# Attention pass: runs of equal destinations marked once in the weighted pass, picks in two bf16 parts, summed and marked by matmuls

## The reference, cut to what matters

```
h = (x @ W).reshape(n, H, C)
a_src, a_dst = sum(h * att_src, -1), sum(h * att_dst, -1)
alpha = leaky_relu(a_src[src] + a_dst[dst], 0.2)
amax  = segment_max(alpha, dst)
ex    = exp(alpha - amax[dst])
out   = segment_sum(h[src] * ex / segment_sum(ex, dst)[dst], dst) + bias
```

## Time and profile before

| what | us |
|---|---|
| median of 3 runs | 10127.84 (10118.32 to 10137.22) |
| span of the profiled execution, first to last instruction | 10186.8 |
| weighted pass in it | 5079 to 6036 |
| attention pass in it | 6126 to 7475 |

### The profile page before, as it was taken

One profiled execution on the slowest core, in us unless ns is written; L12 is line 12 of the kernel. 1 busy time (PEld: TensorE's weight loads), 2 busy tenths in 40 slices (PEclk: granted clock), 3 DMA queues, 4 the chain that ended last, 5 costly groups with the idle time before them and its releaser, 6 DMA issues. The chain is left out here.

```text
span 10186.8 us, 130111 instructions
## 1 busy us (share of the span) xinstructions
PE 5972.5 (59%) x26625; PEld 4680.2 (46%) x26626; DVE 3975.1 (39%) x9144; ACT 2065.8 (20%) x6047; POOL 4999.3 (49%) x5128
## 2 busy tenths in 40 slices
PE   4667666756675667466744673555554564465455
PEld 3556445644564456355633552334443453343344
DVE  4444434443343434344511244556641231222123
ACT  2222222222222212222222233322320000000000
POOL 4554454445445544554455525434326555555655
PEclk8888778877887778787877886767777787787778
DMA  4332332333233322332222215544322222222222
GB/s 122 97 93 89 103 96 84 96 89 98 85 93 93 97 82 84 104 101 86 88 81 72 70 48 188 175 160 157 135 75 85 79 80 84 79 82 76 84 82 77
DMA packets 427779, 980.02 MB, mean 96 GB/s; under 512 B 125761, under 2 KB 205121, under 8 KB 411201
## 3 DMA queue, kind: packets, MB, share of 16 engines
q0 software_dynamic: 245760, 673.51, 22.9%
q1 hardware_dynamic: 124528, 190.17, 5.8%
q10 hardware_dynamic: 57296, 114.45, 3.4%
HBM read 842.61 MB, written 135.14 MB: 96 GB/s over the span
## 5 line engine op out<-in xcount | busy, mean ns | idle before, releaser
L322 POOL DMA_INDIRECT ring<-node_table,idx x4608 | 4474.4, 971 | 4298.1 <-issue 1779.2
L685 PE MATMUL psAT<-ring,S 128*128 128x256 f32 x7600 | 2078.3, 435 | 974.8 <-DVE AGG L847 752.6
L261 DVE SCALAR_TENSOR_TENSOR S<-iota,block_start,dst_f 128x512 f32<-128x512 f32 x1710 | 1280.2, 749 | 2951.4 <-remote 1509.2
L685 PEld LDWEIGHTS psAT<-ring,S 128*128 128x128 f32 x7600 | 1635.6, 221 | 1359.6 <-DVE S L261 717.6
L1026 PE MATMUL psAT<-ring,S 128*128 128x256 f32 x4560 | 1272.9, 440 | 1010.6 <-DVE AGG L1122 679.0
L1026 PEld LDWEIGHTS psAT<-ring,S 128*128 128x128 f32 x4560 | 994.1, 224 | 1293.6 <-issue 983.7
L909 DVE TENSOR_TENSOR ring<-ring,psE 128x256 f32<-128x256 f32 x2560 | 903.4, 415 | 772.6 <-remote 416.3
L779 ACT ACTIVATE ring<-ring 128x256 f32<-128x256 f32 x2560 | 846.3, 408 | 1143.5 <-DVE ring L909 637.5
L1282 POOL DMA_INDIRECT ring<-att_table,idx x512 | 524.0, 1023 | 814.1 <-ACT idx L1480 535.2
L611 PE MATMUL psE<-we_stk,stk 128*128 128x256 bf16 x2560 | 426.8, 302 | 450.8 <-DVE ring L909 217.3
L392 PE MATMUL psAT<-ring,S 128*128 128x256 f32 x1520 | 404.6, 426 | 276.2 <-DVE AGG L474 162.7
(11 more groups left out here) (326 smaller groups left out, 5279.6 us busy)
## 6 DMA issues: line engine op xcount, KB each, us to landing
ring<-node_table,idx POOLq DMA_INDIRECT x4608
rows_table<-ring SPq DMA_DIRECT2D x64, 1072.0 KB
ring<-rows_table ACTq DMA_DIRECT2D x64, 1072.0 KB
stk<-stack_table SPq DMA_DIRECT2D x256, 256.0 KB
node_table<-tab ACTq DMA_DIRECT2D x237, 128.0 KB, 1.9
stack_table<-stk SPq DMA_DIRECT2D x64, 256.0 KB
ring<-att_table,idx POOLq DMA_INDIRECT x512
tT<-in_edge_attr SPq DMA_DIRECT2D x68, 64.0 KB
```

The lines of the kernel that those rows point to most:

```text
L261: nc.vector.scalar_tensor_tensor(S[:, 4 * g:4 * g + 4, :], iota[:, :].unsqueeze(1).to_broadcast([P, 4, P]), block_start[:, bass.ds(blk, 1) ...
L322: nc.gpsimd.indirect_dma_start(ring[:, q, 0:gw], None, table, bass.IndirectOffsetOnAxis(ap=idx[:, q:q + 1], axis=0)).then_inc(gathered[q], 16)
L685: ins = nc.tensor.matmul(psA[:, 0:D], S[:, u, :], ring[:, U * ob + u, 0:D], start=(u == 0), stop=(u == U - 1))
```

## The change

- The marks of the runs are found once, for all 65536 edges, in the weighted pass, and kept in two tables in DRAM. `ends_table` has the destination of every edge that is the last of its run in its tile, and -1 for the others. `run_table` has, for every tile and head, what the scan adds: -1e38 where a run begins, else 0 (8 equal rows for the 8 heads, so 2 MB, written by 8 DMAs). Both are read into `Y` at the start of the attention pass.
- `scan` in the sorted case is the scan alone, from `Y` and from PSUM. The copies, comparisons, the product with `last` and `number` are gone, and PE's two transpositions of `dT` and `lastT` with them.
- The one-hot tiles of `hots` and `further` are made from `run_ends`, so only the last edge of a run is marked in them.
- The picks are two bf16 parts instead of three. A unit of `pick` is 25 matmuls with 8 columns (one that writes the huge negative number everywhere, and per tile one that adds the positive one where a destination is, and one for each part, all into the same 64 columns) instead of 8 with 25.
- `take` is one maximum straight from PSUM and the maximum with `a_max`: 2 instructions instead of 4.
- ACT makes the second `hots` ahead of `exp`.

```diff
@@ attention_pass, sync
+                    sp.dma_start(run_ends, ends_table).then_inc(ends_in, 16)
+                    run_rows = run_table.rearrange("(n q) e -> q n e", q=P)
+                    for n0, n1 in ((0, FIRST), (FIRST, 2 * NG)):
+                        sp.dma_start(edge_runs.rearrange("p (n e) -> p n e", e=P)[:, n0:n1, :],
+                                     run_rows[:, n0:n1, :]).then_inc(runs_in, 16)
                     with sp.Fori(0, NG) as i:
@@ tensor: turn_scores, turn_runs, pick
-                        pe.wait_ge(d16_ready, n + 1)
-                        nc.tensor.transpose(sT, gs[:, P * g:P * g + P], ident[:, :])
-                        nc.tensor.transpose(dT, d16[:, :], ident[:, :]).then_inc(scoresT, 1)
+                        nc.tensor.transpose(sT, gs[:, P * g:P * g + P], ident[:, :]).then_inc(scoresT, 1)
...
-                        nc.tensor.transpose(runT, run[:, :], ident[:, :])
-                        nc.tensor.transpose(lastT, last[:, :], ident[:, :]).then_inc(runsT, 1)
+                        nc.tensor.transpose(runT, run[:, :], ident[:, :]).then_inc(runsT, 1)
...
                             pe.wait_ge(picks_read, c + 1)
+                            nc.tensor.matmul(psV[:, 0:U * PW], ones_b[0:1, :], absent, start=True, stop=False)
                             for u in range(U):
...
-                                ins = nc.tensor.matmul(psV[:, PW * u:PW * u + PW],
-                                                       hot_sets[half if first else 2][:, u, :],
-                                                       picks_b[:, U * half + u, :], start=True, stop=True)
+                                high_low = [picks_b[:, U * half + u, PW * part:PW * part + PW] for part in range(2)]
+                                for part, rhs in enumerate((present, *high_low)):
+                                    ins = nc.tensor.matmul(psV[:, PW * u:PW * u + PW],
+                                                           hot_sets[half if first else 2][:, u, :], rhs,
+                                                           start=False, stop=(u == U - 1 and part == 2))
@@ scalar
                         if picking:
                             hots(2 * n, 0)
+                            hots(2 * n + 1, 1)
                         ahead(i, ob, 1, exp)
-                        if picking:
-                            hots(2 * n + 1, 1)
@@ vector: scan (sorted case), split_picks, take
-                            nc.vector.tensor_tensor(pen[:, :], DT, DTp[:, P - 1:2 * P - 1], ALU.not_equal)
-                            nc.vector.tensor_tensor(last[:, :], DT, DTp[:, P + 1:2 * P + 1], ALU.not_equal)
-                            dve.drain()
-                            nc.vector.tensor_scalar(pen[:, :], pen[:, :], -BIG, None, ALU.mult)
-                            dve.drain()
-                            nc.vector.tensor_tensor_scan(run[:, :], pen[:, :], GT, -BIG, ALU.add, ALU.max)
-                            dve.drain()
-                        nc.vector.tensor_tensor(run[:, :], run[:, :], last[:, :], ALU.mult).then_inc(runs_ready, 1)
-                        number(n + 1)
+                            dve.wait_ge(scoresT, n + 3)
+                            nc.vector.tensor_tensor_scan(run[:, :], own_runs, sT, -BIG, ALU.add, ALU.max
+                                                         ).then_inc(runs_ready, 1)
...
                         nc.vector.tensor_copy(part[0], runs)
-                        nc.vector.tensor_scalar(picks_b[:, :, PW - 1:PW],
-                                                lastT.rearrange("p (t h) -> p t h", h=HEADS)[:, :, 0:1],
-                                                FLAG, None, ALU.mult)
                         dve.drain()
-                        nc.vector.tensor_tensor(rest_f, runs, part[0], ALU.subtract)
-                        dve.drain()
-                        nc.vector.tensor_copy(part[1], rest_f)
-                        dve.drain()
-                        nc.vector.tensor_tensor(part[2], rest_f, part[1], ALU.subtract).then_inc(picks_ready, 1)
+                        nc.vector.tensor_tensor(part[1], runs, part[0], ALU.subtract).then_inc(picks_ready, 1)
...
-                            nc.vector.tensor_reduce(cand[:, :, :], pv[:, :, 0:3 * HEADS].rearrange(
-                                "p u (s h) -> p u h s", s=3), AX.X, ALU.add)
-                            dve.drain()
-                            nc.vector.scalar_tensor_tensor(
-                                cand[:, :, :], pv[:, :, PW - 1:PW].to_broadcast([P, U, HEADS]), FLAG,
-                                cand[:, :, :], ALU.subtract, ALU.add).then_inc(picks_read, 1)
-                            dve.drain()
-                            nc.vector.tensor_reduce(cmax[:, :], cand[:, :, :].rearrange("p u h -> p h u"),
-                                                    AX.X, ALU.max)
+                            nc.vector.tensor_reduce(cmax[:, n, :], pv.rearrange("p u h -> p h u"), AX.X, ALU.max
+                                                    ).then_inc(picks_read, 1)
                             dve.drain()
@@ weighted pass, first work: DVE, PE, SP
+        def find_runs(dve):
+            now, own_fence = numbers[:, :, 0:P], fence[:, :, 1:P]
+            uns = dve.value_load(unsorted_i[0:1, 0:1], min_val=0, max_val=1)
+            dve.wait_ge(numbers_turned, 1)
+            nc.vector.memset(numbers[:, :, P:2 * P], -2.0)
+            nc.vector.tensor_copy(now, turned_numbers)
+            dve.drain()
+            nc.vector.tensor_tensor(ended, now, numbers[:, :, 1:P + 1], ALU.not_equal)
+            dve.drain()
+            with dve.If(uns > 0):
...
+            with dve.Else():
+                nc.vector.memset(fence[:, :, 0:1], -BIG)
+                nc.vector.tensor_scalar(own_fence, ended[:, :, 0:P - 1], -BIG, None, ALU.mult)
+            dve.drain()
+            nc.vector.scalar_tensor_tensor(ended, now, 1.0, ended, ALU.add, ALU.mult)
+            dve.drain()
+            nc.vector.tensor_scalar_add(ended, ended, -1.0).then_inc(ends_made, 1)
+            dve.wait_ge(ends_turned, 1)
+            nc.vector.tensor_copy(now, turned_numbers).then_inc(ends_copied, 1)
+        def store_runs(sp):
+            rows_by_head = run_table.rearrange("(c p h) e -> h p c e", p=P, h=HEADS)
+            sp.wait_ge(ends_made, 1)
+            for h in range(HEADS):
+                sp.dma_start(rows_by_head[h], fence).then_inc(runs_out, 16)
+            sp.wait_ge(ends_copied, 1)
+            sp.dma_start(ends_table.rearrange("p (c e) -> p c e", e=P), numbers[:, :, 0:P]).then_inc(ends_out, 16)
...
```

More of the change, by code:

```diff
@@ L134, in build @@
         ST = stk_f[:, U * P:3 * U * P // 2].bitcast(BF16)
-        run, last, pen = (stk_f[:, n * P:n * P + P] for n in (5, 6, 7))
-        picks = share(MT * (HEADS + 1)).rearrange("p (t h) -> p t h", t=MT)
-        al, cand = (share(U * HEADS).rearrange("p (u h) -> p u h", u=U) for n in range(2))
-        cmax = sb("cmax", [P, HEADS])
+        run, pen = (stk_f[:, n * P:n * P + P] for n in (5, 7))
+        al = share(U * HEADS).rearrange("p (u h) -> p u h", u=U)
+        cmax = share(2 * HEADS).rearrange("p (n h) -> p n h", n=2)
         psE = pb("psE", [P, 4 * 512])
@@ L162, in build @@
         weighed = sem("weighed")
-        d16_ready = sem("d16_ready")
+        numbers_turned, ends_made, ends_turned = sem("numbers_turned"), sem("ends_made"), sem("ends_turned")
+        runs_out, ends_out = sem("runs_out"), sem("ends_out")
+        ends_copied, runs_in, ends_in = sem("ends_copied"), sem("runs_in"), sem("ends_in")
         scoresT = sem("scoresT")
@@ L1220, in attention_pass @@
             offsets = [small2[:, U * n:U * n + U] for n in range(3)]
-            picks_b = scale_row[:, 0:MT * PW // 2].bitcast(BF16).rearrange("p (t w) -> p t w", w=PW)
-            rest_f = flat(picks[:, :, :])[:, 0:P].rearrange("p (t h) -> p t h", h=HEADS)
+            picks_b = scale_row[:, 0:MT * PW].bitcast(BF16).rearrange("p (t w) -> p t w", w=2 * PW)
+            edge_runs = Y[:, 0:2 * NG * P]
+            run_ends = Y[:, 2 * NG * P:2 * NG * P + NT]
+            marks, ones_b = (rows[:, 1, P // 2 * n:P // 2 * n + P // 2].bitcast(BF16) for n in range(2))
+            present, absent = marks[:, 0:PW], marks[0:1, PW:PW + U * PW]
+            FIRST = 4
             FLAG = 2.0 ** 126
@@ L1303, in _ @@
                     sp.sem_inc(octet_free, NO)
+                    sp.wait_ge(ends_in, 16)
+                    sp.wait_ge(runs_in, 32)
                     loads(sp)
@@ L1553, in _ @@
                     load(0, 1)
+                    act.wait_ge(ends_in, 16)
                     hots(0, 0)
@@ L1854, in _ @@
                     dve.drain()
-                    number(0)
+                    dve.wait_ge(ends_in, 16)
+                    dve.wait_ge(runs_in, 32)
                     for n in range(2):
@@ L2433, in turned_weight, with turn_numbers @@
```

(39 more changed lines are left out.)

47 lines of the change are left out of this document (21 added, 26 removed).

## The result

The changed kernel takes 10055 us (median of 4 runs) against 10123 for the kernel before, run beside it: ratio 0.9934, 95% interval 0.991 to 0.9957, some 67 us less. 10031 had been predicted. One thing has to be known for all that follows: the chips were of two kinds. On one the kernel before takes 9950 to 10125 us (the first pair and e4 to e7, e10, e11), on the other 7785 (e0 to e3, e8, e9). I call them the slow kind and the quick kind, and compare inside a kind only. Runs that stand on different chips of one kind are compared by their ratios to the kernel before, which ran beside each of them.

A forecast was written before the change was run, and what follows sets the result against it. DVE's program, run nearly serially, was taken to bound the attention pass. Scan and split -57, takes -49, picks +11, second hots -5, weighted pass +3 gave -97 us: 10127.84 - 97 = 10031 us, range 9975 to 10100.

The forecast's parts named there:

- The bound: Attention loop: DVE's program, run nearly serially, sets the pace, its 687 busy us and 244 of waits making 931 of 1175.
- Scan and split, 57 us: DVE in picking steps: shorter scan and split save 2.6 us in first and 1.2 in second steps, over 15 turns.
- freed time turns into waits: Rival, attention loop: PE's sums are late whenever runs are turned, scan and split give nothing; -40 us, 10088; 16%.
- Takes and picks, 49 - 11 + 5 = 43 us: Attention loop: shorter takes on DVE gain 49 us, PE's longer picks lose 11, second hots ahead of exp gain 5.
- the rival of 0.096 us each: PE's picks: weight loads can't overlap, a unit's pick takes 2.4 us instead of 0.36; 10152 us; 9%.
- The third rival: DVE's attention loop, about 100 instructions shorter, no longer needs its instructions brought each turn; 55 us more gained, 9976; 10%.
- Its 3 us: Weighted pass: `find_runs` and the run table lose 3 us, bounds 0 and 27, mostly covered by DVE's wait for gathered rows.
- The prediction's own sign of being wrong: Attention loop: picking steps lose under 1.5 us each, or row waits at L1783 grow by what the steps lose.

The follow-up runs named there:

- e4: The kernel before the change, unchanged, run once for its trace on a slow-kind chip: 10125.33 us.
- e7: The changed kernel with 64 register moves on DVE ahead of the attention loop: 10076.96 us, 0.9951 of the kernel before.
- e10: The changed kernel with the take's maximum read eight times over in the same number of instructions: 9914.92 us, 0.9958 of the kernel before.
- e11: The changed kernel with PE turning the runs earlier in second picking steps and DVE splitting behind the exponents: 9890.88 us, 0.9929 of the kernel before.
- e0: The changed kernel again, unchanged, on a quick-kind chip: 7664.35 us against 7784.5 for the kernel before, 0.9839.
- e3: The changed kernel with the earlier four-instruction take and eight-matmul pick (17 columns, two parts): 7727.47 us, 0.9925 of the kernel before.
- e8: The changed kernel with 9 matmuls in a pick instead of 25, mark and low part left out: 7646.21 us, 0.9815 of the kernel before.
- e9: The changed kernel with a take of four DVE instructions again, PE's pick as changed: 7724.14 us, 0.9918 of the kernel before.
- e6: The changed kernel with 49 matmuls in a pick instead of 25, the 24 added ones with zeros: 10124.54 us, 0.9989 of the kernel before.
- e1: The changed kernel with ACT copying the next indices behind exp in picking steps, so gathers begin later: 7680.85 us, 0.9863 of the kernel before.

## Why the prediction came out as it did

*The bound.* That DVE's nearly serial program sets the pass holds, with one exception, on the slow kind: at the first take of a picking step the signal that comes with the end of the gathers does.

*Scan and split, 57 us.* The section came out as worked out. From the rescaling to the exponents first steps lost 2.4 us and second ones 1.1 (2.6 and 1.2 predicted), 52 in all, with the wait for PE in second steps that was foreseen (2.5 us). The failed step is the next one, which the prediction took without saying so: that what is gained ahead of the first take comes through it. 27 us did not. The row was there: the earlier trace rows has 68.5 us of L1665 until "remote". I read these stalls as instructions being fetched and used them for a rival only. They were waits for PE's signal, and on the slow kind such a wait ends 2 to 3 us behind the last gather's issue, so a DVE that comes sooner waits longer. The rival "freed time turns into waits" named the right outcome with the wrong wait, PE's late sums.

*Takes and picks, 49 - 11 + 5 = 43 us.* Behind the first take the steps lost 41 (and 41 from e3 to e0 on the quick kind: 1.62 in first, 1.29 in second steps). The take is 0.22 + 0.2 + 0.17 us, as predicted, and two of one octet start 1.29 us apart instead of 1.41. The sum is right by two errors. The picks were sized too low: 16 matmuls are worth 18 us (e8), where 11 stood for 17, because a DVE that is faster by the same change waits for PE more often (49 times at L1658 instead of 16). If the picks cost these 19, the takes brought 41 + 19 = 60 rather than 49. e9 shows 33 of it (60 less the 27 at L1736) for DVE's work alone; the rest isn't separated. On the slow kind 24 more matmuls cost 55 (e6).

*Weight loads.* The 25 matmuls of a unit start within 0.9 us (6597.28 to 6598.0), 0.025 us apart at 8 columns, and in e0 PE's semaphore follows such a record by 0.01 us, so the rival of 0.096 us each is out. The Trainium skill, TensorE: Matmul & The Clock Gate, section "Part 2: What happens when you issue a matmul", has both figures: its floor of about 25 ns agrees, its load time did not set the pace here.

*DVE's loop.* Not in the sum: one packet of instructions a turn fewer, and with it 1.45 us in every first step, 22 us. The third rival looked at the program's length too, but its own step failed: the wait at the loop's turn stayed (61.4 and 66.7 us), and the packets still come each turn. The Trainium skill, Runtime: NRT & Kernel Launch, section "Instruction fetch mechanics", gives PE four times the room of the other engines and calls a fetch in sequence mostly hidden. That PE's longer program brought no packet agrees with the first (e6). If the 1.5 us are the wait for this one packet, it was not hidden here, which does not agree with the second.

*The other steps* of the turn became 18 us longer (8 to 10 against e4), at L1736 and at the loop's turn. The waits at these sums in the kernel before differ by 9 us between its own two traces (15.9 and 25.3), so half of it need not be the change's. I can't name the cause of the rest.

*Weighted pass.* `find_runs` took 5.7 us on DVE, which then idled 17.67, so it was covered; the pass took 941 us, against 957 in the first trace of before and 931 in e4's. Its 3 us can't be seen beside these 26. From the first scan to the first weighing 4 to 6 us were lost (55.8 and 54.0 to 60.1 and 58.9).

```profile
5061.16 0.48 DVE L2438 MEMSET w_odd<- 128x512 f32 x1 [0.89 <-issue]
...
5066.20 0.69 DVE L2460 COPY w_odd<-psV 128x512 f32<-128x512 f32 x1 [1.21 <-PE psV L2465]
...
5095.17 0.42 DVE L476 TENSOR_TENSOR AGG<-AGG,psAT 128x256 f32 x1 [17.67 <-remote]
```

The ledger of the loop, first trace against the trace after: over 14 turns DVE is ready for the first take 63 us sooner (49 from scan and split, 20 from the packet, 6 lost in between), 27 are given back in the wait, 41 are gained behind it, 4 in the first turn, and 18 are lost in the other steps: -63 + 27 - 41 - 4 + 18 = -63. On the quick kind nothing is given back, and the change brings 120, more than the 97 predicted.

*How much of it was luck.* On the slow kind the total of 67 lies in the range, but the 20 us of the packet, which no term had, stand against the 27 given back in the wait, which no term had either. The prediction's own sign of being wrong, picking steps that lose under 1.5 us each, was nearly met: first steps lost 3.9 us and second ones 1.7 (3.1 and 1.5 against e4), where 2.5 to 4 had been named. The 120 us of the quick kind are above the 97, and the prediction has no term for such a chip.

What stays open: why PE is late while gathers run on one kind of chip. That the two go together is in every trace of the slow kind; to move the gathers was tried on the other kind only (e1), so that the gathers hold PE is argued from the times, not shown by an edit. Whether the signal or the matmuls are late can't be told from the first trace, since the ends of matmuls are modelled; in e6 the records themselves come 1.43 us apart and the signal follows the last of them at once, which speaks for PE itself being held. Each chip was used in one session, so whether the kind is the chip's own or a state that it was in isn't shown either.

## What to carry to other kernels

A wait that the profile can't name is still a wait: before summing what is saved ahead of it, see what its end coincides with, here the last gather of a burst, and count only what moves that. Count a loop's instructions as well as their durations, since here a program shorter by one packet of instructions a turn came with 22 us less, beside what its instructions took. And price added work on a second engine by the waits as they will be once the first engine is faster, not as they are.

## What the runs showed of the hardware

- The kernel before takes 7785 us on two chips and 9950 to 10125 on others. Packets last alike: a gather's 4096 bytes have a median of 159 ns on both, and ACT's and SP's rows of 8576 bytes 324.
- On the slow kind PE's semaphore is raised up to 6 us behind the record of a pick's last matmul while POOL gathers (the changed kernel, first turn left out), 2.2 to 3.1 us behind the last gather's issue; single register instructions last 0.70 to 0.73 us instead of 0.04 to 0.2, and matmuls come 1.43 us apart in the worst stretches (e6). On the quick kind the signal follows the record by 0.01 us (e0) and none of the rest was seen.
- PE's granted clock was 0.79 to 0.80 on the slow kind and 0.86 to 0.87 on the quick one.
- Where DVE's loop brings 7 packets of 8 KB of instructions a turn (before, e3, e4, e9), a turn's first step is 1.1 to 1.9 us longer to the end of the rescaling than where it brings 6 (all the others); 64 instructions ahead of the loop (e7) and longer work in as many instructions (e10) change neither.
